# The merged sweep's five picks placed further apart in a chunk, and the comparisons for the next chunk moved into its middle

## The chip, the cores and the metric

The kernel runs on one core of one Trainium2 chip. The metric is the time of one execution on the device in microseconds (us). TensorE (PE in the rows) does matmuls, VectorE (DVE) and ScalarE (ACT) elementwise work, GpSimd (POOL) issues the indirect gathers, SyncE (SP) the plain transfers.

## What is computed

A graph of 6250 nodes and 100000 edges, sorted by their target node, goes through four layers, each followed by a residual sum and a layer norm: a spline network with its convolution, three attention layers, two graph convolutions, and three hops of neighbour means. The change lies in the spline convolution at the end of the first layer. For every edge the edge's place is shifted by the difference of a value of its two nodes and clipped, and the eight corners of the cell that it falls into are weighted:

```python
new_pseudo = jnp.clip(pseudo + t[col] - t[row], 0.0, 1.0)
basis2, idx2 = spline_basis(new_pseudo)
return spline_conv(x, row, col, basis2, idx2, conv_w, conv_b)
...
z = jnp.einsum('ni,kio->nko', x, W).reshape(N * K, Fout)
gathered = z[col[:, None] * K + idx]
msg = jnp.einsum('es,eso->eo', basis, gathered)
out = jax.ops.segment_sum(msg, row, num_segments=N)
```

## The kernel before

Edges lie as 128 partitions times 784 columns. The stage of the change, `stage_conv_sweep`, does two things at a time over chunks of 14 columns (`ch`), two chunks (ring buffers, `b` 0 and 1) a step, 28 steps, so 56 chunks.

**The sweep proper.** GpSimd issues 14 indirect gathers a chunk (line 1885) that fetch each edge's block of the table `z_conv` into `ring[b]`. VectorE multiplies four pairs of corners with their weights (line 2164), adds them up in three steps (2175 and 2176, 2186 and 2187, 2197: the sums), adds the carry of the chunk before (2199) and runs a scan along the columns (2212). ScalarE writes the result out. After the sums VectorE frees the ring (`ring_free`); ScalarE then copies the indices of the chunk two further on (`stage`, 1959), and GpSimd, which waits for them on line 1883, gathers into the ring again.

**The look-up, three steps ahead.** For each edge the value t of one of its nodes is fetched by one-hot products. VectorE makes two one-hot tiles for a chunk (`make`, two comparisons: `hot_lo`, line 2030, and `hot_hi`, 2032). The 14 columns of a chunk are done in five units of three (the last of two). For a unit TensorE counts and turns the one-hots (`turn`, 1910 and 1911), ScalarE copies the turned rows (`take_rows`, 1950), TensorE multiplies them with the table in three parts (`look`, 1920), and VectorE picks the wanted column out of the product (`pick`, 2039, which waits on line 2038). Two result banks alternate, so look u needs pick u-2 to be over (`found_free`). TensorE's order in a chunk is written out: turn 0; then for each row copy that is ready, turn u and look u-1. ScalarE's order in a chunk: the five row copies, the staging of the next indices, the corner weights, then, after the scan (`sums_ready`), the decay factors, the copy out, and the next chunk's row copies.

A third thread, the edge's new place (`place_...`: lines 2046 to 2097), is cut into small steps that stand between the others on VectorE; in even chunks it begins with a long sum (2046).

VectorE's order is written out in `chunk` (2136 on). Ahead of the loop, six chunks of look-ups run alone (`looks_of`), while the first 28 gathers go. The loop has 50 chunks with look-ups; six chunks without follow. Before the change the one-hots are made at the end of a chunk, for the chunk two further on, into the tiles that this chunk's picks have just left.

Of the kernel before, what the change touches and what calls it, by code (L numbers as in the profile page):

```python
# [8 lines left out]
ALU = mybir.AluOpType  # L9
# [5 lines left out]
P = 128  # L15


def gnn_stack_kernel(nc, t, out, stop=None):
# [41 lines left out]
    def sem(name):  # L60
        if name not in sems:
            sems[name] = ctx.enter_context(nc.semaphore(name))
        return sems[name]
# [32 lines left out]
    with ctx:  # L96
# [20 lines left out]
        dve_step, act_step, pe_step, pool_step = (sem(n) for n in ("dve_step", "act_step", "pe_step", "pool_step"))  # L117
# [1704 lines left out]
        def stage_conv_sweep(z, units_, tt, spread, pseudo, key, deg, keep, run, tail):  # L1822
# [10 lines left out]
            with ExitStack() as st, nc.Block() as block:  # L1833
# [71 lines left out]
                def _(pe):  # L1905
# [34 lines left out]
                    pe.wait_ge(sem("hot_made"), 2)  # L1940
                    pe.sem_inc(sem("hot_made"), -2)
# [74 lines left out]
                def _(v):  # L2016
# [12 lines left out]
                    def make(parity, col):  # L2029
                        v.tensor_tensor(hot_lo[parity][:, :, :], short[:, bass.ds(col, ch)].unsqueeze(1).to_broadcast([P, P, ch]),  # L2030
                                        number[:, :, :], ALU.is_equal)
                        v.tensor_tensor(hot_hi[parity][:, :, :], digits[:, bass.ds(col, ch)].unsqueeze(2).to_broadcast([P, ch, NT]),
                                        iota[:, 0:NT].unsqueeze(1).to_broadcast([P, ch, NT]), ALU.is_equal).then_inc(sem("hot_made"), 1)
# [8 lines left out]
                    def pick_on(b, u):  # L2042
                        pick(b, u).then_inc(sem("found_free"), 1)
# [102 lines left out]
                    def chunk(it, b, looks, places):  # L2146
# [15 lines left out]
                        for n in range(4):  # L2162
                            wgt = wgt8[b][:, :, 2 * n:2 * n + 2].unsqueeze(3).to_broadcast([P, ch, 2, fo])
                            last = v.tensor_tensor(acc[n] if n < 2 else pair[n], pair[n], wgt, ALU.mult)
                        last.then_inc(dve_step, 1)
# [5 lines left out]
                        if looks:  # L2171
                            pick_on(b, 0)
                        v.wait_ge(dve_step, 1)
# [8 lines left out]
                        if looks:  # L2182
                            pick_on(b, 1)
# [9 lines left out]
                        if looks:  # L2193
                            pick_on(b, 2)
# [4 lines left out]
                        v.scalar_tensor_tensor(sums[b][:, :, 0], tail[:, :], keep[:, bass.ds(col, 1)], sums[b][:, :, 0], ALU.mult, ALU.add).then_inc(dve_step, 1)  # L2199
                        if places:  # L2200
                            if b == 0:
                                place_cell(1)
                            else:
                                place_index(0, place_col)
                        if looks:
                            pick_on(b, 3)
# [3 lines left out]
                        v.sem_inc(sem("decay_ready"), -1)  # L2210
                        flat = sums[b][:, :, :].rearrange("p f j -> p (f j)")
# [6 lines left out]
                        if looks:  # L2218
                            pick_on(b, 4)
# [3 lines left out]
                        v.tensor_copy(tail[:, :], sums[b][:, :, ch - 1]).then_inc(dve_step, 1)  # L2223
# [5 lines left out]
                        v.wait_ge(dve_step, 1)  # L2229
                        v.sem_inc(dve_step, -1)  # L2230
                        if looks:
                            make(b, look_col + (2 + b) * ch)
                        if places:
                            if b == 0:
                                place_share(1)
                            else:
                                place_end(place_col)

# [5 lines left out]
                    make(1, AHEAD * GR + ch)  # L2244
# [1258 lines left out]
```

## Time and profile before

| | us |
|---|---|
| median of 3 runs | 11738.81 |
| lowest and highest run | 11734.01, 11827.18 |
| profiled execution | 11728.26 |
| its span | 11726.5 |
| VectorE busy in the span | 5526.4 |
| GpSimd busy in the span | 6027.4 |
| TensorE busy in the span | 3555.6 |

The stage of the change takes some 1400 us of the span, from 5107 to 6510; the chain of work through it is what is read below. A row of the order of time gives the start from the beginning of the span and the duration in us, the engine, the line, the operation, output and inputs, and in brackets how long the engine was idle before it and what ended that. "DVEq L2038" is VectorE's own queue at line 2038, which waits there.

### The profile page before, as it was taken

The page shows a single profiled execution, that of the slowest core. Times are in us where ns is not written, and L with a number is a line of the kernel's source. Part 1 is how long each engine was busy: PE and PEld are TensorE (multiplying, and loading weights), DVE is VectorE, ACT ScalarE, POOL GpSimd, SP SyncE. Part 2 cuts the span into 40 slices and gives each one's busy share as a digit, 9 for nine tenths or more (in the row PEclk, how much of TensorE's full clock was granted, in tenths as well). Part 3 has the DMA queues.
Part 4 walks back from the last instruction along what each step waited for, and adds up shares of the span by engine and source line. Part 5 has one row for each costly group of instructions (what it writes and reads, how often), then busy time and mean ns, then how long its engine had stood idle before and what let it go on. Part 6 is the DMA issues. An engine that isn't in the chain of part 4 may idle for free. (4 is left out here: it accounts for less than half of the span.)

```text
span 11726.5 us, 86679 instructions
## 1 busy us (share of the span) xinstructions
PE 3555.6 (30%) x19657; PEld 2292.8 (20%) x19713; DVE 5526.4 (47%) x8114; ACT 2549.8 (22%) x3835; POOL 6027.4 (51%) x6000
## 2 busy tenths in 40 slices
PE   4334310266344443343332100010000200036787
PEld 3222200243111111132222100010000100023554
DVE  5333358444666666557677322222222588871201
ACT  0212125244233333211111011110111244430000
POOL 1555557400565666536656577757776566640000
PEclk8555555588555555555555555555555555558899
DMA  7000012299799999725555111111111132328798
GB/s 297 2 2 2 2 44 103 91 390 391 299 368 357 370 366 369 271 56 143 145 142 151 46 35 32 34 26 36 34 32 33 38 99 99 99 70 310 284 412 356
DMA packets 582791, 1887.74 MB, mean 161 GB/s; under 512 B 253627, under 2 KB 315490, under 8 KB 552065
## 3 DMA queue, kind: packets, MB, share of 16 engines
q0 software_dynamic: 305264, 762.32, 20.7%
q1 hardware_dynamic: 234592, 722.30, 15.9%
q10 hardware_dynamic: 42784, 401.43, 8.2%
q8 instruction: 55, 0.90, 0.0%
q14 instruction: 96, 0.79, 0.0%
HBM read 1170.21 MB, written 715.38 MB: 161 GB/s over the span
## 5 line engine op out<-in xcount | busy, mean ns | idle before, releaser
L2314 POOL DMA_INDIRECT ring<-tab_gat,at x2352 | 2348.5, 999 | 902.3 <-issue 851.9
L735 POOL DMA_INDIRECT ring<-z_stn,at x784 | 761.5, 971 | 1293.3 <-POOLq L742 758.0
L580 POOL DMA_INDIRECT sorted<-rows,at x784 | 799.7, 1020 | 777.1 <-POOLq L578 540.8
L1558 PE MATMUL pair_acc<-pair_x_w,pair_cell 32*112 32x384 f32 (+1 forms) x1120 | 781.0, 879 | 1128.2 <-remote 489.1
L1885 POOL DMA_INDIRECT ring<-z_conv,at x784 | 806.5, 1029 | 599.4 <-POOLq L1883 367.4
L2893 PE MATMUL acc<-spot,ones 128*128 128x128 f32 x6 | 2.3, 487 | 3419.3 <-PEq L2282 2243.7
L1305 PE MATMUL acc<-tile,parts 128*96 128x448 f16 (+1 forms) x3430 | 727.6, 361 | 251.6 <-DVE parts L1229 138.7
L2425 DVE COPY peak<-peak 128x6 f32<-128x6 f32 x112 | 20.0, 179 | 1557.9 <-DMA ring<-tab_gat,at 1341.9
L2893 PEld LDWEIGHTS acc<-spot,ones 128*128 128x128 f32 x6 | 1.5, 310 | 3420.0 <-issue 3420.0
L1558 PEld LDWEIGHTS pair_acc<-pair_x_w,pair_cell 32*112 32x112 f32 x1120 | 317.1, 295 | 1591.1 <-issue 1584.4
L2349 ACT ACTIVATE weights_bank<-arg 128x168 f32<-128x168 f32 (+1 forms) x112 | 31.3, 279 | 2391.3 <-issue 2000.1
L2461 DVE TENSOR_TENSOR_SCAN sums<-decay,sums 128x1176 f32<-128x1176 f32 (+1 forms) x112 | 517.3, 4619 | 29.0 <-issue 15.8
L1305 PEld LDWEIGHTS acc<-tile,parts 128*96 128x96 bf16 (+1 forms) x3430 | 404.3, 125 | 568.9 <-DMA tile<-adj 233.5
L743 POOL DMA_INDIRECT adj<-pair_val,pair_at x392 | 412.0, 1051 | 193.5 <-issue 103.5
L2448 DVE TENSOR_TENSOR sums<-ring,weights_bank 128x1008 f32<-128x1008 f32 (+1 forms) x112 | 430.0, 3839 | 133.7 <-issue 96.7
L1138 POOL DMA_INDIRECT adj<-val_a,at_a x392 | 387.4, 988 | 189.9 <-issue 127.3
L1211 POOL DMA_INDIRECT own<-tab_gcn,ex_src x5 | 5.6, 1120 | 905.5 <-DMA tab_gcn<-hop 599.9
L1676 PE MATMUL planes<-wsb,turned 64*128 64x384 f32 (+1 forms) x1960 | 420.9, 557 | 124.8 <-PEq L1672 116.2
L1693 DVE COPY block<-planes 128x384 f32<-128x384 f32 x588 | 296.0, 552 | 335.1 <-DVEq L1712 335.1
L2364 ACT COPY out_rows<-sums 128x1176 f32<-128x1176 f32 (+1 forms) x112 | 443.0, 3955 | 48.7 <-ACTq L2363 18.6
L1920 PE MATMUL found<-parts,lo_rows 128*128 128x147 bf16 x2352 | 322.0, 313 | 392.9 <-PEq L1917 322.1
L1595 ACT COPY pair_block<-pair_acc 112x384 f32<-112x384 f32 (+1 forms) x896 | 380.0, 501 | 239.9 <-ACTq L1591 107.6
(540 smaller groups left out, 10202.4 us busy)
## 6 DMA issues: line engine op xcount, KB each, us to landing
tile<-adj SPq DMA_DIRECT2D x490, 784.0 KB, 21.4
z_stn<-block ACTq DMA_DIRECT2D x98, 2400.0 KB
z_conv<-pair_block ACTq DMA_DIRECT2D x224, 700.0 KB
run_gat<-out_rows SPq DMA_DIRECT2D x56, 1596.0 KB
adj<-zero SPq DMA_DIRECT2D x49, 1568.0 KB
run_basis<-out_rows SPq DMA_DIRECT2D x28, 1750.0 KB
ring<-tab_gat,at POOLq DMA_INDIRECT x2352
run_gat<-out_rows SPq DMA_DIRECT2D x56, 672.0 KB
```

The source lines that it names most:

```text
L580: g.indirect_dma_start(out=dest, out_offset=bass.IndirectOffsetOnAxis(ap=at[b][:, k:k + 1], axis=0), in_=rows[b][:, k, :], in_offset=None) ...
L735: g.indirect_dma_start(out=view(bufs[b], k), out_offset=None, in_=table, in_offset=bass.IndirectOffsetOnAxis(ap=at[n][b][:, k:k + 1], axis ...
L743: g.indirect_dma_start(out=adj, out_offset=bass.IndirectOffsetOnAxis(ap=pair_at[b][:, k // 2:k // 2 + 1], axis=0), in_=pair_val[b][:, k // ...
L1138: g.indirect_dma_start(out=adj, out_offset=bass.IndirectOffsetOnAxis(ap=at_a[:, k:k + 1], axis=0), in_=val_a[:, k:k + 1], in_offset=None). ...
L1305: ins = pe.matmul(acc[0:3 * w, b, 0:HW_B], parts[:, t_, :, :].rearrange("p k f -> p (k f)"), self.ring[n % RING][:, b * HW_B:(b + 1) * HW_ ...
L1558: last = pe.matmul(self.acc[g][0:self.nodes, n, 0:(hi - lo) * self.fo], self.cell[:, :], cols, start=True, stop=True)
L1676: ins = pe.matmul(self.acc[g][:, n, 0:(hi - lo) * self.fo], self.turned[rows, k, :], cols, start=True, stop=True)
L1885: g.indirect_dma_start(out=ring[b][:, k, :, :, :].rearrange("p u s o -> p (u s o)"), out_offset=None, in_=z, in_offset=bass.IndirectOffset ...
L2314: g.indirect_dma_start(out=ring[b][:, k, :], out_offset=None, in_=tab_gat, in_offset=bass.IndirectOffsetOnAxis(ap=at[b][:, k:k + 1], axis= ...
L2364: a.copy(out_rows[b][:, :, 0:n_sums], sums[b][:, :, :, :].rearrange("p h f j -> p j (h f)"))
L2448: v.tensor_tensor(sums[b][:, :, 1:per_head, :], val_of(ring[b]), ex.unsqueeze(2).to_broadcast([P, NH, width, ch]), ALU.mult)
L2461: v.tensor_tensor_scan(flat, decay[:, :, :, :].rearrange("p h f j -> p (h f j)"), flat, 0.0, ALU.mult, ALU.add).then_inc(dve_step, 1)
```

## The change

VectorE's order in `chunk` is written anew; nothing is computed otherwise, and the four other engines keep their order (TensorE's last wait takes one announcement of one-hots instead of two). The one-hots are made for the next chunk instead of the one after it, in front of the scan instead of at the chunk's end; the pair that stood ahead of the loop for the second chunk goes. The picks move: pick 0 stands after two of the four multiplications, pick 1 after the other two, pick 2 behind the sums, pick 3 behind the one-hots, pick 4 behind the scan's announcement.

```diff
@@ -1937,8 +1937,8 @@
                     with pe.Fori(0, steps):
                         for b in range(2):
                             chunk(b)
-                    pe.wait_ge(sem("hot_made"), 2)
-                    pe.sem_inc(sem("hot_made"), -2)
+                    pe.wait_ge(sem("hot_made"), 1)
+                    pe.sem_inc(sem("hot_made"), -1)
                     pe.matmul(counts_, none[:, :], hot_hi[0][:, 0, :], start=False, stop=True).then_inc(sem("all_counted"), 1)
 
                 @block.scalar
@@ -2159,10 +2159,9 @@
                         acc = [near[:, :, n, :, :] for n in range(2)]
                         if places and b == 0:
                             place_sum()
-                        for n in range(4):
-                            wgt = wgt8[b][:, :, 2 * n:2 * n + 2].unsqueeze(3).to_broadcast([P, ch, 2, fo])
-                            last = v.tensor_tensor(acc[n] if n < 2 else pair[n], pair[n], wgt, ALU.mult)
-                        last.then_inc(dve_step, 1)
+                        wgt = [wgt8[b][:, :, 2 * n:2 * n + 2].unsqueeze(3).to_broadcast([P, ch, 2, fo]) for n in range(4)]
+                        v.tensor_tensor(acc[0], pair[0], wgt[0], ALU.mult)
+                        v.tensor_tensor(acc[1], pair[1], wgt[1], ALU.mult)
                         if places:
                             if b == 0:
                                 place_add(place_col)
@@ -2170,6 +2169,10 @@
                                 place_share(0)
                         if looks:
                             pick_on(b, 0)
+                        v.tensor_tensor(pair[2], pair[2], wgt[2], ALU.mult)
+                        v.tensor_tensor(pair[3], pair[3], wgt[3], ALU.mult).then_inc(dve_step, 1)
+                        if looks:
+                            pick_on(b, 1)
                         v.wait_ge(dve_step, 1)
                         v.sem_inc(dve_step, -1)
                         v.tensor_tensor(acc[0], acc[0], pair[2], ALU.add)
@@ -2179,8 +2182,6 @@
                                 place_sub(place_col)
                             else:
                                 place_two()
-                        if looks:
-                            pick_on(b, 1)
                         v.wait_ge(dve_step, 1)
                         v.sem_inc(dve_step, -1)
                         v.tensor_tensor(acc[0][:, :, 0, :], acc[0][:, :, 0, :], pair[3][:, :, 0, :], ALU.add)
@@ -2190,24 +2191,26 @@
                                 place_clip()
                             else:
                                 place_weights(place_col)
-                        if looks:
-                            pick_on(b, 2)
                         v.wait_ge(dve_step, 1)
                         v.sem_inc(dve_step, -1)
                         step(v.tensor_tensor(sums[b][:, :, :].rearrange("p f j -> p j f"), acc[0][:, :, 0, :], pair[3][:, :, 1, :], ALU.add))
                         v.sem_inc(sem(f"ring_free{b}"), 1)
                         v.scalar_tensor_tensor(sums[b][:, :, 0], tail[:, :], keep[:, bass.ds(col, 1)], sums[b][:, :, 0], ALU.mult, ALU.add).then_inc(dve_step, 1)
+                        if looks:
+                            pick_on(b, 2)
                         if places:
                             if b == 0:
                                 place_cell(1)
                             else:
                                 place_index(0, place_col)
                         if looks:
-                            pick_on(b, 3)
+                            make(1 - b, look_col + (1 + b) * ch)
                         v.wait_ge(dve_step, 1)
                         v.sem_inc(dve_step, -1)
                         v.wait_ge(sem("decay_ready"), 1)
                         v.sem_inc(sem("decay_ready"), -1)
+                        if looks:
+                            pick_on(b, 3)
                         flat = sums[b][:, :, :].rearrange("p f j -> p (f j)")
                         v.tensor_tensor_scan(flat, decay[:, :, :].rearrange("p f j -> p (f j)"), flat, 0.0, ALU.mult, ALU.add).then_inc(dve_step, 1)
                         if places:
@@ -2215,33 +2218,30 @@
                                 place_cell(2)
                             else:
                                 place_index(1, place_col)
-                        if looks:
-                            pick_on(b, 4)
                         v.wait_ge(dve_step, 1)
                         v.sem_inc(dve_step, -1)
                         v.sem_inc(sem("sums_ready"), 1)
-                        v.tensor_copy(tail[:, :], sums[b][:, :, ch - 1]).then_inc(dve_step, 1)
                         if places:
                             if b == 0:
                                 place_cell(3)
                             else:
                                 place_index(2, place_col)
-                        v.wait_ge(dve_step, 1)
-                        v.sem_inc(dve_step, -1)
                         if looks:
-                            make(b, look_col + (2 + b) * ch)
+                            pick_on(b, 4)
+                        v.tensor_copy(tail[:, :], sums[b][:, :, ch - 1]).then_inc(dve_step, 1)
                         if places:
                             if b == 0:
                                 place_share(1)
                             else:
                                 place_end(place_col)
+                        v.wait_ge(dve_step, 1)
+                        v.sem_inc(dve_step, -1)
 
                     make(0, 0)
                     for n in range(AHEAD):
                         looks_of(n)
                         if n + 1 < AHEAD:
                             places_of(n)
-                    make(1, AHEAD * GR + ch)
                     with v.Fori(0, steps - AHEAD) as it:
                         for b in range(2):
                             chunk(it, b, True, True)
```

The row numbers of lines differ by one or a few in the changed kernel; the names are the same (`found_245` and `found_246` are the two result banks, `hot_hi_222` and `hot_hi_223` the one-hots of even and odd chunks, `ring_236` and `sums_238` belong to the odd chunk). VectorE's first half of an odd chunk in the loop, from the multiplications to the additions of pairs, before:

```order
L2164 TENSOR_TENSOR corner_banks<-ring_236,corner_banks 128x14x64 x2
L2164 TENSOR_TENSOR ring_236<-ring_236,corner_banks 128x14x64 x2
L2072 TENSOR_SCALAR share<-share 128x84
L2039 TENSOR_TENSOR prod<-found_246,hot_hi_223 128x441
L2175 TENSOR_TENSOR corner_banks<-corner_banks,ring_236 128x14x64
L2176 TENSOR_TENSOR ring_236<-corner_banks,ring_236 128x14x64
L2076 TENSOR_TENSOR two<-share 128x112
L2039 TENSOR_TENSOR prod<-found_245,hot_hi_223 128x441
```

The same place in the changed kernel:

```order
L2163 TENSOR_TENSOR corner_banks<-ring_236,corner_banks 128x14x64
L2164 TENSOR_TENSOR corner_banks<-ring_236,corner_banks 128x14x64
L2072 TENSOR_SCALAR share<-share 128x84
L2039 TENSOR_TENSOR prod<-found_246,hot_hi_223 128x441
L2172 TENSOR_TENSOR ring_236<-ring_236,corner_banks 128x14x64
L2173 TENSOR_TENSOR ring_236<-ring_236,corner_banks 128x14x64
L2039 TENSOR_TENSOR prod<-found_245,hot_hi_223 128x441
L2178 TENSOR_TENSOR corner_banks<-corner_banks,ring_236 128x14x64
L2179 TENSOR_TENSOR ring_236<-corner_banks,ring_236 128x14x64
```

Picks 0 and 1 (line 2039) each moved up past two large operations. VectorE's second half of an odd chunk, from the weights of the third thread to the chunk's last row copies, before:

```order
L2091 TENSOR_TENSOR w_231<-two,share 128x224
L2039 TENSOR_TENSOR prod<-found_246,hot_hi_223 128x441
L2197 TENSOR_TENSOR sums_238<-corner_banks,ring_236 128x14x32
L2199 ISA
L2199 SCALAR_TENSOR_TENSOR sums_238<-conv_tail,keep_s,sums_238 128x32
L2081 ISA
L2081 SCALAR_TENSOR_TENSOR spot<-cell,base 128x28
L2039 TENSOR_TENSOR prod<-found_245,hot_hi_223 128x441
L2212 SCALAR_TENSOR_TENSOR sums_238<-decay,sums_238 128x448
L2084 SCALAR_TENSOR_TENSOR spot<-cell,spot 128x28
L2039 TENSOR_TENSOR prod<-found_246,hot_hi_223 128x294
```

After these stand the carry's copy (2223) and the two comparisons, there for `hot_lo_221` and `hot_hi_223`, the odd chunk's own tiles. The same place in the changed kernel:

```order
L2196 TENSOR_TENSOR sums_238<-corner_banks,ring_236 128x14x32
L2198 ISA
L2198 SCALAR_TENSOR_TENSOR sums_238<-conv_tail,keep_s,sums_238 128x32
L2039 TENSOR_TENSOR prod<-found_246,hot_hi_223 128x441
L2081 ISA
L2081 SCALAR_TENSOR_TENSOR spot<-cell,base 128x28
L2030 ISA
L2030 TENSOR_TENSOR hot_lo_220<-short_b,number_b 128x1792
L2032 ISA
L2032 TENSOR_TENSOR hot_hi_222<-digits,iota 128x686
L2039 TENSOR_TENSOR prod<-found_245,hot_hi_223 128x441
L2215 SCALAR_TENSOR_TENSOR sums_238<-decay,sums_238 128x448
```

Pick 2 moved from ahead of the sums to behind them, and the comparisons, now for the next (even) chunk's tiles, stand between pick 2 and pick 3, ahead of the scan (line 2215).

## Rows read from the trace of the kernel before

**Rows 1.** Windows: length; PE, PEld, DVE, ACT, POOL busy; clock, DMA; then L2030 alone.

```profile
5223.00:6396.00 1173.00, 387.99 (x3424) 337.55 (x3424) 827.51 (x1301) 208.22 (x441) 709.93 (x687) 0.54 0.51 144
6396.00:6505.00 109.00, 0.20 (x1) 0.10 (x1) 67.61 (x92) 11.07 (x21) 69.17 (x70) 0.50 0.56 160
...
5223.00:6396.00 1173.00, 53.52 (x49) 0.54 0.51 144
```

**Rows 2.** Waits, 5223 to 6396: who for whom; us in total, times, longest.

```profile
POOL ring L1885 <- POOLq L1883: 314.4, 50, 54.2
...
DVE prod L2039 <- DVEq L2038: 287.4, 57, 9.6
```

**Rows 3.** Order of time, VectorE, an even chunk, its successor's beginning and pick 2.

```profile
5543.70 2.08 DVE L2164 TENSOR_TENSOR ring<-ring,corner_banks 128x896 f32<-128x896 f32 x2
...
5545.85 0.61 DVE L2039 TENSOR_TENSOR prod<-found,hot_hi 128x441 f32<-128x441 f32 x1
...
5548.52 0.62 DVE L2039 TENSOR_TENSOR prod<-found,hot_hi 128x441 f32<-128x441 f32 x1
...
5550.11 0.20 DVE L2058 TENSOR_SCALAR moved<-moved 128x84 f32<-128x84 f32 x1
5554.91 0.62 DVE L2039 TENSOR_TENSOR prod<-found,hot_hi 128x441 f32<-128x441 f32 x1 [4.60 <-DVEq L2038]
5555.45 0.91 DVE L2197 TENSOR_TENSOR sums<-corner_banks,ring 128x448 f32<-128x448 f32 x1
...
5557.00 0.61 DVE L2039 TENSOR_TENSOR prod<-found,hot_hi 128x441 f32<-128x441 f32 x1
5557.53 1.08 DVE L2212 TENSOR_TENSOR_SCAN sums<-decay,sums 128x448 f32<-128x448 f32 x1
...
5559.61 1.09 DVE L2030 TENSOR_TENSOR hot_lo<-short_b,number_b 128x1792 bf16<-128x1792 bf16 x1 [0.24 <-DVEq L2230]
...
5561.41 0.24 DVE L2070 SCALAR_TENSOR_TENSOR share<-moved,cell 128x84 f32<-128x84 f32 x1
...
5579.18 0.62 DVE L2039 TENSOR_TENSOR prod<-found,hot_hi 128x441 f32<-128x441 f32 x1 [8.84 <-DVEq L2038]
```

**Rows 4.** Order of time, TensorE, looks 0 to 2 of the odd chunk.

```profile
5562.28 1.32 PE L1920 MATMUL found<-parts,lo_rows 128*128 128x147 bf16 x9
...
5563.84 1.22 PE L1920 MATMUL found<-parts,lo_rows 128*128 128x147 bf16 x9
...
5566.42 0.75 PE L1920 MATMUL found<-parts,lo_rows 128*128 128x147 bf16 x9 [0.95 <-DVE prod L2039]
```

**Rows 5.** Order of time, GpSimd, first, second and last gather, next first.

```profile
5533.73 1.51 POOL L1885 DMA_INDIRECT ring<-z_conv,at  x1 [5.39 <-POOLq L1883]
5535.54 1.85 POOL L1885 DMA_INDIRECT ring<-z_conv,at  x1 [0.30 <-issue]
...
5551.45 0.94 POOL L1885 DMA_INDIRECT ring<-z_conv,at  x1 [0.30 <-issue]
5557.95 1.42 POOL L1885 DMA_INDIRECT ring<-z_conv,at  x1 [5.56 <-POOLq L1883]
```

**Rows 6.** The gathers' line, 5133 to 5170: ns min/median/max, first and last start.

```profile
L1885 POOL DMA_INDIRECT ring<-z_conv,at x28: 942/946/1325, 5133.2 to 5167.3; - x28
```

**Rows 7.** Order of time, VectorE, the four picks that follow, ahead of the loop.

```profile
5137.74 0.62 DVE L2039 TENSOR_TENSOR prod<-found,hot_hi 128x441 f32<-128x441 f32 x1 [1.10 <-DVEq L2038]
5143.51 0.62 DVE L2039 TENSOR_TENSOR prod<-found,hot_hi 128x441 f32<-128x441 f32 x1 [5.15 <-DVEq L2038]
5156.23 0.62 DVE L2039 TENSOR_TENSOR prod<-found,hot_hi 128x441 f32<-128x441 f32 x1 [12.10 <-DVEq L2038]
5169.52 0.47 DVE L2039 TENSOR_TENSOR prod<-found,hot_hi 128x294 f32<-128x294 f32 x1 [12.67 <-remote]
```

**Rows 8.** Order of time, ScalarE, row copies 0 and 4 of the odd chunk.

```profile
5561.10 0.48 ACT L1950 CAST lo_rows<-turned 128x384 bf16<-128x384 f32 x1 [0.35 <-ACTq L1949]
...
5579.92 0.37 ACT L1950 CAST lo_rows<-turned 128x256 bf16<-128x256 f32 x1 [8.08 <-ACTq L1949]
```

## The prediction

> **What bounds the kernel now.** The change touches one stage, the merged sweep of the first graph layer, so I read that stage alone: first busy times by stretch, then the waits inside it, then single chunks in order of time. The loop that the change rewrites takes 1173 us for 49 chunks [rows 1], 23.94 us each, and VectorE is busy for 827.51 us of it, 16.9 us a chunk. In the list of waits VectorE's largest is the pick, 287.4 us in 57 waits that line 2038 ends, where it waits for a look (the product on TensorE) to be announced; GpSimd waits 314.4 us for its indices, 54.2 of them before the loop's first chain of gathers [rows 2], so 5.3 us a chunk. Neither engine is full, and each chunk loses some 6 us of VectorE in front of a pick.
>
> The order of time tells which pick, and why. In the chunk at 5543 picks 0 and 1 come without a wait (5545.85 and 5548.52), and pick 2 starts after 4.60 us of idleness, at 5554.91; in the next chunk pick 2 waits 8.84 us, to 5579.18 [rows 3]. Yet TensorE's row of look 2 in that chunk ends at 5566.42 + 0.75 = 5567.17 [rows 4]: it is announced 12 us after its row. What ends the wait is seen on GpSimd: the first gathers of the two chains start at 5533.73 and 5557.95, and the two late picks start 21.18 and 21.23 us after them, 2.5 us after the last of the 14 gathers (5551.45 + 0.94 = 5552.39) [rows 3, 5]. The stretch before the loop shows the same beside an idle VectorE: 28 gathers run from 5133.2 to past 5167.3 [rows 6], 1.26 us apart, and picks that only follow one another come at 5137.74, 5143.51, 5156.23 and 5169.52 [rows 7], that is 4.5, 10.3, 23.0 and 36.3 us after the first gather, with up to 12.67 us of waiting, where the rows of two looks in a row are 1.56 us apart (5562.28, 5563.84) [rows 4]. I read from this: **TensorE's announcements pass at once in the first 6 us or so after a chain of gathers has begun, are held afterwards with one let through now and then, and all pass about 21.2 us after its first gather.** That is the bound of a chunk: gathers, release, what is left on VectorE, the next gathers.
>
> That row and announcement differ is nothing odd in itself. The Trainium skill, "Perfetto Trace Analysis", section "Per-instruction lifecycle: what the profiler-reported window actually captures", says that a matmul's end in a profile is an estimate, while its semaphore follows PSUM's acknowledgement; the 12 us agree with the order, but no page read gives a reason for the size.
>
> **The change, part by part.**
>
> *Work.* The loop issues the same instructions a chunk. One pair of comparisons less runs ahead of the loop, 1.80 us (5559.61 to 5561.41) [rows 3]: -2 us.
>
> *Picks.* Now picks 0, 1 and 2 stand before the sums (line 2197) that free the ring and so let ScalarE stage the next indices; after, only picks 0 and 1 do. If looks came at the same times as now, the wait of pick 2 would no longer hold the ring.
>
> *The comparisons, from behind the scan to before it.* They and pick 2 will stand between the freeing of the ring and the scan. Now it is 1.55 us from the start of the sums to pick 3 (5555.45 to 5557.00), 0.91 of them the sums, then pick 3 0.53 and the scan 1.08 [rows 3]. After: 0.64 + pick 2 0.53 + a gap of 0.24 + comparisons 1.80 + pick 3 0.53 + scan 1.08 = 4.82 us from the end of the sums to the end of the scan. The next first gather comes 1.59 us after the sums (5556.36 to 5557.95) [rows 3, 5]. So the scan will end 3.2 us after the first gather; now it is 5558.61 - 5557.95 = 0.66 us. **This step decides.** ScalarE waits for the scan, copies the chunk out, and only then turns to the next chunk's row copies: copy 0 starts 2.49 us after the scan (5558.61 to 5561.10) [rows 3, 8], and every look of the next chunk stands behind it.
>
> *Where the looks fall then.* Now copy 0 is 3.15 us after the first gather, look 0's row ends 2.5 us after the copy's start (5562.28 + 1.32 = 5563.60), and look 1's 1.5 us later [rows 4]: 5.6 and 7.1 us after the first gather, in time for VectorE; look 2 ends 9.2 us after it and is held to 21.2. After the change copy 0 comes at 3.2 + 2.49 = 5.7, look 0 at 8.2 and look 1 at 9.7 or later: both in the held stretch. Bounds: let through in the middle, as what released the pick at 10.3 [rows 7], or held to 21.2, as look 2 now. Turn 1 and look 0 are issued before turn 2 and look 1, and in rows 7 the next one to pass after 10.3 passed at 23.0. So I take look 0 in the middle and look 1 held.
>
> *A chunk then.* Pick 1 at 21.2; the pick, two additions and a placing step as from pick 0 to pick 1 now, 2.67 us (5545.85 to 5548.52); the two half additions, 1.59 - 0.53 = 1.06 (5548.52 to 5550.11, less a pick); a placing step 0.20 and the sums 0.91 [rows 3]: 4.84. Then 1.59 to the next first gather. 21.2 + 4.84 + 1.59 = 27.6 us; and since the ring sets the gathers again, the next scan ends 3.2 us after them too, so the state keeps itself up. Against 23.94 that is +3.66, times 49 = **+179 us**.
>
> *The comparisons beside the gathers.* Now the gather that meets them takes 1.85 us where others take 0.95 [rows 5]. After, they start about 1.4 us after the sums and still run into the first two gathers, so these 0.9 us stay; were they to fall away, it would be 49 x 0.9 = 44 us less. The Trainium skill, "SBUF — State Buffer", section "Who interferes with whom", infers that a two-input VectorE operation leaves descriptor generation alone; the 1.85 us beside one speak against it. By the rule the 44 us could not be in the sum at all, and moving the comparisons would be free.
>
> *Sum.* Span 11726.5 + 179 - 2 = 11903.5; 1.8 us lie around the span (11728.26). The median of the runs is 10.6 above the profiled one, so **11915 us**, +1.5%.
>
> **The rivals.**
>
> 1. *Look 0 is held to the end too* (the 23.0 in rows 7 speaks for it, the 10.3 against). Pick 0 at 21.2 and 0.53, two multiplications 2.08 [rows 3], pick 1 at 23.8: a chunk of 30.2, +6.3 x 49 = +307: 12040 us.
>
> 2. *Look 1 is let through in mid-chunk.* Then the ring is free early and the row copies set the pace: copy 4 comes with the release (0.7 us after the pick in its chunk, 5579.92 to 5579.18 [rows 3, 8], or with it), its 0.37 and 1.59 us of staging follow: 23.2 to 23.9 a chunk, 0 to 0.7 less than now: 11700 to 11740, or up to 11810 where look 1 passes only at 19 us (19 + 4.84 + 1.59 = 25.4 a chunk). For it: something passes in mid-chunk now as well, or copy 4 would come later than the release; against it: look 1 is the fourth thing issued, not the second.
>
> 3. *Faster:* the hold hangs on how TensorE and VectorE alternate, not on the gathers, and spreading the picks dissolves it. Then gathers set the chunk: in the last six chunks, which have no looks, 109 us or 18.2 each [rows 1], or 14 x 1.26 + 2 = 19.6. (23.94 - 19.6) x 49 = -213: 11525 us. Against it stand rows 7, where VectorE does nothing and the hold is there. It is decided by look 2: out by 14 us after the first gather, or not. The same section of the Trainium skill says that TensorE and ScalarE never wait on anyone, which would be this case; the held picks show that the announcements do wait, if not at SBUF's ports.
>
> **How the numbers follow.** Look 1 held: 0.50. Rival 1: 0.12. Rival 2: 0.29. Rival 3: 0.09. About 1% (117 us, 2.4 us a chunk) is what a measurement of this kernel can tell from no change: the first two cases lie beyond it (0.62), rival 2 within. The range from 11700 to 12040 leaves out rival 3 and what exceeds rival 1. The likeliest case alone has 11855 to 11980 (look 1 out at 20 to 22.5 us).
>
> **What would show it.** In the trace after: VectorE's wait moves from pick 2 to pick 1 (the pick behind line 2173), about 10 us long, ending 21 us after the first gather; the scan ends some 3 us after the first gather; GpSimd's wait for indices grows from 5.3 to some 9 us a chunk; picks 2 to 4 have no wait. I am wrong if the scan ends less than 2 us after the first gather, or if looks whose rows end 8 to 10 us after the first gather are announced at once.

## The result, and the profile after

The changed kernel takes 11897.42 us (median of 3 runs, 11892.09 to 11920.31) against 11738.81: 158.6 us more. The ratio over the runs is 1.0102, 95% interval 1.0057 to 1.0147, so it is slower, by less than 2%; it lies below that of the medians (1.0135) because the three runs of before spread over 93 us. Timed a second time, beside the experiments, it was 1.0155 (1.0118 to 1.0191).

The profiled execution of after is the longest of its three (11920.31 us, span 11918.5). Its span is 192.0 longer than that of before: 158.7 of it between the first and the last gather of the merged sweep (1511.7 us, before 1353.0), 7.8 ahead of it, 25.5 behind it, where the two programs are the same. The sweep's share comes out at the difference of the medians; that it does so to a tenth of a us is chance, since these are single executions. In the second pair of traces the sweep is 145.3 us longer (1477.8 and 1332.5).

The loop of after, by windows (columns as in [rows 1]), and the waits inside it:

```profile
5230.00:6561.00 1331.00, 397.95 (x3424) 341.21 (x3424) 836.77 (x1298) 207.86 (x441) 675.75 (x686) 0.53 0.46 127
```

```profile
POOL ring L1885 <- POOLq L1883: 496.6, 49, 52.8
DVE prod L2039 <- DVEq L2038: 388.5, 80, 9.4
```

1331 us in place of 1173 [rows 1] for 49 chunks: 27.2 us each, while VectorE's work hardly grew (836.77 against 827.51). GpSimd's waits for indices went from 5.3 to 9.2 us a chunk ((496.6 - 52.8) / 48), VectorE's waits for a look from 287.4 [rows 2] to 388.5 us.

One odd chunk in order of time, VectorE (start, length, line, out<-in, idle before and what ended it):

```profile
5552.28 0.92 DVE L2196 TENSOR_TENSOR sums<-corner_banks,ring 128x448 f32<-128x448 f32 x1
...
5553.73 0.61 DVE L2039 TENSOR_TENSOR prod<-found,hot_hi 128x441 f32<-128x441 f32 x1
...
5554.36 1.08 DVE L2030 TENSOR_TENSOR hot_lo<-short_b,number_b 128x1792 bf16<-128x1792 bf16 x1
5555.36 0.87 DVE L2032 TENSOR_TENSOR hot_hi<-digits,iota 128x686 bf16<-128x686 f32 x1
5556.15 0.61 DVE L2039 TENSOR_TENSOR prod<-found,hot_hi 128x441 f32<-128x441 f32 x1
5556.67 1.08 DVE L2215 TENSOR_TENSOR_SCAN sums<-decay,sums 128x448 f32<-128x448 f32 x1
...
5566.66 0.62 DVE L2039 TENSOR_TENSOR prod<-found,hot_hi 128x441 f32<-128x441 f32 x1 [5.05 <-DVEq L2038]
...
5575.28 0.62 DVE L2039 TENSOR_TENSOR prod<-found,hot_hi 128x441 f32<-128x441 f32 x1 [6.01 <-DVEq L2038]
...
5579.41 0.92 DVE L2196 TENSOR_TENSOR sums<-corner_banks,ring 128x448 f32<-128x448 f32 x1
```

The same chunk on GpSimd (first, second and last gather, next first), ScalarE (row copies 0 to 3) and TensorE (looks 0 and 1):

```profile
5554.79 1.48 POOL L1885 DMA_INDIRECT ring<-z_conv,at  x1 [9.21 <-POOLq L1883]
5556.57 0.95 POOL L1885 DMA_INDIRECT ring<-z_conv,at  x1 [0.30 <-issue]
...
5571.55 0.94 POOL L1885 DMA_INDIRECT ring<-z_conv,at  x1 [0.30 <-issue]
5581.80 1.58 POOL L1885 DMA_INDIRECT ring<-z_conv,at  x1 [9.31 <-POOLq L1883]
```

```profile
5560.23 0.48 ACT L1950 CAST lo_rows<-turned 128x384 bf16<-128x384 f32 x1 [0.35 <-ACTq L1949]
5561.75 0.48 ACT L1950 CAST lo_rows<-turned 128x384 bf16<-128x384 f32 x1 [1.04 <-ACTq L1952]
5573.07 0.48 ACT L1950 CAST lo_rows<-turned 128x384 bf16<-128x384 f32 x1 [10.84 <-ACTq L1949]
5575.33 0.48 ACT L1950 CAST lo_rows<-turned 128x384 bf16<-128x384 f32 x1 [1.78 <-ACTq L1949]
```

```profile
5561.42 1.32 PE L1920 MATMUL found<-parts,lo_rows 128*128 128x147 bf16 x9
...
5562.98 1.12 PE L1920 MATMUL found<-parts,lo_rows 128*128 128x147 bf16 x9
```

What to see: the scan ends at 5557.75, 2.96 us after the first gather (before 0.66); copy 0 starts at 5.4. Looks 0 and 1 end at 5562.74 and 5564.10 by their rows, 7.95 and 9.3 us after the first gather. Pick 0 gets its look at 11.9 and pick 1 at 20.5 us, 11 us after look 1's row and 2.8 us after the last gather's end (5572.49). (In the even chunks pick 0 waits less: a median 1.6 us, against 3.6 in the odd.) Behind pick 1 come the sums, and 1.5 us behind these the next gathers: 27.0 us. Picks 2 to 4 wait for nothing, here and in every other chunk of the loop.

### The profile page after: what moved, and what is told of

The parts are those of the page before. It is cut to its first block and busy times, and to the rows that moved or that the text cites. A ratio compares the mean times of both kernels' runs of the same rounds, so it can differ in the third digit from the quotient of the medians.

```text
span 11918.5 us, 86677 instructions
## 1 busy us (share of the span) xinstructions
PE 3576.1 (30%) x19657; PEld 2303.2 (19%) x19713; DVE 5535.9 (46%) x8112; ACT 2549.3 (21%) x3835; POOL 6000.1 (50%) x6000
## 3 DMA queue, kind: packets, MB, share of 16 engines
q0 software_dynamic: 305264, 762.32, 21.2%
q1 hardware_dynamic: 234592, 722.30, 15.6%
## 5 line engine op out<-in xcount | busy, mean ns | idle before, releaser
L1885 POOL DMA_INDIRECT ring<-z_conv,at x784 | 772.7, 986 | 792.1 <-POOLq L1883 558.9
L2364 ACT COPY out_rows<-sums 128x1176 f32<-128x1176 f32 (+1 forms) x112 | 443.1, 3956 | 48.7 <-ACTq L2363 15.6
## 6 DMA issues: line engine op xcount, KB each, us to landing
tile<-adj SPq DMA_DIRECT2D x490, 784.0 KB, 21.4
```

Source lines behind the costliest of these rows:

```text
L1885: g.indirect_dma_start(out=ring[b][:, k, :, :, :].rearrange("p u s o -> p (u s o)"), out_offset=None, in_=z, in_offset=bass.IndirectOffset ...
L2364: a.copy(out_rows[b][:, :, 0:n_sums], sums[b][:, :, :, :].rearrange("p h f j -> p j (h f)"))
```

## The experiments

**My theory:** GpSimd's chain of gathers holds TensorE's announcements; the change makes the looks late against the chain, because the scan ends later. **Rivals:** the picks' new places cost it by themselves; the hold comes from the bytes moved, or from how TensorE and VectorE alternate. The experiments ran on several chips (the kernel before took 11640 to 11769 us there), so ratios are against the kernel before timed beside each; they all differ from 1 by some 2% or less, and what counts is whether the interval leaves out 1. Chunk means are of the profiled execution, from the sums of one chunk on VectorE to the sums of the next.

### Is it the gathers? Seven of them, and none (e5, e6)

```
e5:  for k in range(7): g.indirect_dma_start(...)          # was range(ch), 14
   + g.dma_start(ring[b][:, 7:ch], z[0:P*7*(KD+2), :] in pieces of one gathered row)
e6:  no indirect gather; one g.dma_start for all 14
```

> The changed kernel with seven indirect gathers a chunk in place of 14; the other seven rows of a chunk come by one plain transfer of the same size and the same pieces from fixed rows, issued by GpSimd behind them (their indices are left out of the computation). My theory: the hold goes with GpSimd's chain of gathers, so it ends some 2.8 us after the seventh: 7 x 1.25 + 0.5 + 2.8 = 12 us after the first gather in place of 20.5, and a chunk is 12 + 4.84 + 1.59 = 18.4 us or what VectorE's 17.6 us of work and short waits make it, up to 20; about 11430 to 11520 us with the last six chunks shorter too. The rivals: the hold goes with the bytes moved or with how TensorE and VectorE alternate: pick 1 stays some 20 us after the first gather, 27 us a chunk, 11850 or more.

> The changed kernel with all 14 gathers of a chunk replaced by one plain transfer of the same bytes in the same pieces from fixed rows (the indices are left out of the computation). My theory: without indirect gathers no announcement is held; every look is out within 0.5 us of its row's end, no pick waits over 3 us, and VectorE's work sets the chunk, 17.6 to 20 us: 11400 to 11520 us. If it is the bytes that hold TensorE, picks still wait 5 us or more while the transfer runs. If TensorE's rows are simply shown too early and the looks take that long by themselves, the picks wait as in the changed kernel, 27 us a chunk.

Measured: 11527.6 and 11433.07 us, one run each, beside one of 11769.23 for the kernel before. A chunk is 20.1 and 18.9 us; e5 lies just above what was expected of it (11520 us, 20 us a chunk), e6 within. VectorE's waits for looks in the loop (who for whom, us, times, longest), first e5, then e6, and the window of e6:

```profile
DVE prod L2041 <- DVEq L2040: 87.1, 24, 3.7
```

```profile
DVE prod L2038 <- DVEq L2037: 30.7, 24, 1.3
```

```profile
5195.00:6105.00 910.00, 364.14 (x3360) 317.95 (x3360) 816.54 (x1272) 203.58 (x432) 51.99 (x48) 0.58 0.51 181
```

388.5 us of waiting became 87.1 and 30.7, and VectorE is busy 816.54 of 910 us in e6: it now sets the chunk. The bytes do not hold TensorE: e6 moves 181 GB/s where the changed kernel moves 127. Nor do TensorE and VectorE by themselves: their work and order are unchanged. For every turn and look of the loop I took the time from the end of its row to the change of its semaphore in the trace, grouped by when the row ended, in us after the chain's first gather (in e6 after the transfer's issue); count: median/longest:

```
       0 to 4         6 to 8         8 to 10           10 to 14        14 to 20       20 to 24
after  96: 0.01/0.02  72: 0.04/3.80  120: 10.08/12.31  1: 8.43/8.43    51: 3.95/7.42  131: 0.01/0.47
e5     96: 0.01/0.02  72: 0.03/2.41  120:  1.68/2.08   129: 0.01/0.02  63: 0.01/0.02  -
e6     96: 0.01/0.02  48: 0.01/0.02  128:  0.01/0.26   175: 0.01/0.26  33: 0.01/0.02  -
```

The same instructions at the same distance are late by 10.08, 1.68 and 0.01 us with 14, 7 and 0 gathers. (Nine rows of after end later than 24 us; they are late by 0.02 at most.) A chunk of e5, GpSimd's seventh gather and VectorE's picks 0 and 1 (first gather at 5523.11):

```profile
5531.16 0.95 POOL L1885 DMA_INDIRECT ring<-z_conv,at  x1 [0.30 <-issue]
```

```profile
5533.53 0.62 DVE L2041 TENSOR_TENSOR prod<-found,hot_hi 128x441 f32<-128x441 f32 x1 [3.62 <-DVEq L2040]
5536.06 0.61 DVE L2041 TENSOR_TENSOR prod<-found,hot_hi 128x441 f32<-128x441 f32 x1
```

Pick 0 comes 1.4 us after the seventh gather's end, pick 1 without a wait. The theory stands for what holds. What in the gathers does it, no run shows: GpSimd's work of issuing them, their packets (in the trace of after the last of a chain ends a median 0.4 us before look 1 is announced), or their completions, one for each gather where the plain transfer has one for all. Nor does a run show whether the product itself or only its announcement is late: a row's end is modelled, and TensorE goes on with its next rows meanwhile (turn 2 starts at 5562.53 in the chunk shown above, with look 0 not announced before 5566.5).

### Which part of the change costs? (e1, e2, e3)

```
e1 (after):   make(1-b) taken from ahead of the scan; make(b), two chunks ahead, at the end
e2 (before):  make(b) taken from the end; make(1-b), one chunk ahead, ahead of the scan
e3 (after):   pick 2, make, pick 3 moved from ahead of the scan to behind it
```

> The changed kernel, but with the comparisons back at the chunk's end, two chunks ahead; the picks stay where the change puts them. My theory: what costs is that the scan ends 3 us after the first gather. Here 1.8 us of comparisons leave the stretch between the sums and the scan, so the scan ends 1.2 to 1.4 us after the first gather, copy 0 comes at 3.7 to 3.9, look 0's row ends at 6.3 and look 1's at 7.8. Look 0 still passes at once, look 1 is the first or the second announcement that is held: out at 11.7 or 18.2 us after the first gather (as looks 0 and turn 2 in the changed kernel), so the ring is free early or at 23.0; a chunk of 23.3 to 24.6 us, 11710 to 11790 us. The rival, that the places of the picks cost it and not the comparisons: a chunk stays at 27.0 us and the time at 11900.

> The kernel before with its picks, but the comparisons between the sums and the scan, one chunk ahead. My theory: the scan ends 2.5 to 3 us after the first gather, all looks come as late as in the changed kernel, look 1 is announced at 20.5 us and look 2 only 1 to 1.5 us behind it; pick 2 stands before the sums, so a chunk is 21.5 to 22 + 0.5 + 0.9 + 1.6 = 24.5 to 25.0 us, up to 27 where pick 1 at 20.5 has the two half additions behind it too; 11770 to 11890 us, slower than before in any case. The rival, that the places of the picks alone cost it: 23.9 us a chunk, 11740.

> The changed kernel with its two picks ahead of the sums and one-ahead comparisons, but the scan straight behind the sums and picks 2 to 4 and the comparisons behind the scan. My theory: the scan ends 0 to 0.5 us after the first gather or before it, copy 0 comes at 3 us or earlier, looks 0 and 1 pass at once as in the kernel before, nothing held stands in front of the sums; the ring is free at about 15 us, and the next indices wait only for ScalarE's row copy 4 (turn 4, at about 21): first gather at 23.2 to 23.9, 11700 to 11740 us, no slower than before and 160 to 200 us faster than the changed kernel. The rival, that two picks ahead of the sums cost it wherever the scan is: 27 us a chunk, 11900.

| run | ratio to before (95%) | chunk (sums to sums): mean, shortest to longest | scan's end after the first gather, median |
|---|---|---|---|
| before, two traces | 1 | 23.94, 21.3 to 25.1; 23.55, 17.8 to 36.2 | 0.66; 0.66 |
| after, again | 1.0155 (1.0118 to 1.0191) | 26.5, 24.1 to 27.0 | 2.97 |
| e1 | 1.0035 (1.0022 to 1.0048) | 24.0, 15.7 to 44.8 | 0.89 |
| e2 | 1.0092 (1.0064 to 1.0121) | 25.2, 24.6 to 25.6 | 2.45 |
| e3 | 1.0000 (0.9978 to 1.0021) | 23.15, 18.0 to 36.2 | -3.7 |

A chunk of e3 in a steady stretch, its first gather, scan and the next first gather (the scan ends at 5640.81, 3.45 us ahead of that gather):

```profile
5622.25 1.13 POOL L1885 DMA_INDIRECT ring<-z_conv,at  x1 [4.65 <-POOLq L1883]
5639.72 1.09 DVE L2209 TENSOR_TENSOR_SCAN sums<-decay,sums 128x448 f32<-128x448 f32 x1 [0.16 <-issue]
5644.26 1.33 POOL L1885 DMA_INDIRECT ring<-z_conv,at  x1 [4.58 <-POOLq L1883]
```

The comparisons ahead of the scan cost 0.9% by themselves, the picks' places 0.35%. With both but the scan moved forward (e3) nothing is lost: the rival on the picks' places is wrong for the most part, and what costs is the late scan. By their means all three came out as expected (e2 0.2 us above the 24.5 to 25.0 given first, e3 just below 23.2), but not in their course. From sums to sums, chunks of 24 us did not stay 24:

```
after   27.0 27.0 27.1 27.0 27.1 27.1 28.6 27.0 27.0 27.0 27.0 26.9 27.1 27.0 28.5
e1      18.3 27.8 18.9 28.5 18.9 29.2 15.7 26.6 27.7 22.3 21.6 27.7 18.2 30.4 15.7
e3      18.7 29.4 18.7 22.1 20.8 23.5 18.3 27.6 19.4 24.9 20.8 23.5 20.8 23.5 18.0
before  19.8 26.2 21.1 24.8 22.6 24.0 22.0 24.8 23.3 24.0 24.0 24.0 24.0 24.0 19.9
```

(the last line is the second trace of before). Most of this is not the clock of the loop: the sums move inside a chain, according to which look is held, while ScalarE stages the next indices only behind row copy 4, whose turn mostly comes with the release. In the first six chunks of e1 above, the sums start some 16 and some 21 us after the first gather by turns, but the first gathers lie 22.6 to 24.2 us apart. From first gather to first gather the loop of the second trace of before has 22.8 to 24.1 us in all but four of its 49 chunks, and e3 21.9 to 26.6. A chunk grows much longer where a chain follows the one ahead almost at once: three chains in these traces (two in the second of before, one in e1) begin 0.3 to 2.1 us after the last gather, in place of some 5. Row copy 0 then comes 6.8, 20.8 and 21.7 us after the first gather, in place of some 3, and these chunks take 27.7, 35.3 and 39.9 us.

e3 has steady stretches of 22.0 to 22.4 and chunks of up to 26.6, and its mean is 0.4 to 0.8 below before's two traces, 20 to 39 us, of which the times show nothing. For the second trace of before I expected

> The kernel before, unchanged, for a second trace of it beside the others of this call. My theory: the same chunk as in the first trace, 23.9 us; if a chunk here is 23.0 to 23.3, single executions of the kernel before differ by as much as the scan-first kernel gains.

(11695.04 us, 23.55 us a chunk: single executions of before differ by half of what e3 has on the first), and for that of after

> The changed kernel, unchanged, timed beside the others. 27.0 us a chunk again, and 1.010 to 1.016 times the kernel before.

(26.5 us a chunk where 27.0 was expected, and a ratio of 1.0155.)

### Trying to keep the gain (e4, e7 to e10)

e3's steady 22.1 us a chunk invite edits that start the next gathers right with the release, or bring copy 0 sooner.

```
e4 (e3):   ScalarE: wait turned(4); [ring_free; stage]; copy 4            # stage was behind copy 4
e7 (e3):   ScalarE: copy 3; [ring_free; weights; decay; copy-out]; wait turned(4); copy 4; stage
e8 (e7):   stage ahead of copy 4, as in e4
e9 (e3):   GpSimd: ahead of gather 7 of 14 wait for ScalarE's row copy 1;  e10: for row copy 3
```

> The kernel of e3 with one edit on ScalarE: the next indices are staged when turn 4 is announced, ahead of row copy 4, not behind it. My theory: the release of turn 4 at 20.5 to 21.2 us after the first gather then sets the next gathers 1.2 us later: a chunk of 21.7 to 22.4 us, 75 to 110 us less than the kernel before: 11630 to 11665 us. If instead the announcements are held longer when the gathers follow one another more closely (as ahead of the loop, one in 12.7 us), turn 4 comes later and the chunk is 24 us or more: 11740 or above.

> The kernel of e3 with ScalarE's weights, decay, copy-out ahead of the wait for turn 4, where ScalarE stands idle, and the next indices behind row copy 4 as in e3. In e3's trace a chunk alternates: 22.1 us where looks 0 and 1 come early, and 27 to 36 where copy 0 came late and they were held. Here copy 0 of the next chunk has only row copy 4 and the staging ahead of it on ScalarE, and turn 0: 1.0 to 1.5 us after the first gather in place of 2.1 in e3. My theory (announcements pass in the first 6 us): looks 0 and 1 pass in nearly every chunk, chunks of 22.0 to 22.5 with every eighth 1.4 us longer, mean 22.3 to 23.0: 0.992 to 0.998 times the kernel before. If the hold does not go by the time since the first gather, the long chunks stay: mean 23.1 and no less than e3's time.

> The kernel of e7 with the next indices staged when turn 4 is announced, ahead of row copy 4, as in e4. The first gather then comes 0.5 to 0.7 us sooner after the release, and copy 0 1.6 to 2.1 us after it. My theory: chunks of 21.5 to 22.0 where looks 0 and 1 still pass, mean 21.7 to 22.8, 0.990 to 0.997 times the kernel before; if that 0.6 us already makes them late, as e4 against e3, long chunks of 29 to 32 come back and the mean is 24: 1.00 or above.

> The kernel of e3 with one edit: after the seventh gather of a chain GpSimd waits until ScalarE has made row copy 1 of the running chunk. My theory (the hold ends 2.6 us after a chain's last gather, and only then): where copy 1 has passed early nothing changes; where it is held, seven gathers end at 8.8 us, turn 1 is announced at 11.4, the second seven run from 11.9 to 20.7, and the looks pass in the 6 us from 11.4 on; the ring is free at about 20 and the next chain begins at 21.3 to 22: mean chunk 21.3 to 22.8, 0.983 to 0.996 times the kernel before. If a pause inside the chain ends no hold, each chunk is some 3 us longer: 24 to 27 us, 1.00 to 1.02 times.

> The kernel of e9 with the pause in the middle of a chain tied to row copy 3, which the traces show held, not to copy 1, which mostly passes early. My theory (a hold ends some 2.6 us after GpSimd's last gather, also of half a chain): seven gathers end 9 us after the first, turn 3 is announced at 11 to 12 us, the second seven run until 20.7 to 21.5, turn 4 and the looks pass in the 6 us from 11.4 on, the ring is free at about 16 to 20 and the next chain follows at once: mean chunk 21 to 22.5 us, 0.983 to 0.996 times the kernel before. If a pause inside the chain ends no hold, GpSimd stands until one announcement is let through in mid-chain: 24 to 29 us a chunk, 1.00 to 1.03.

Measured, ratio to before and mean chunk: e4 1.0043 (1.0025 to 1.0062), 24.2; e7 1.0098 (1.0062 to 1.0135), 24.7; e8 1.022 (1.0181 to 1.0259), 27.8; e9 1.0031 (1.0013 to 1.0049), 23.9; e10 1.0004 (0.9991 to 1.0017), 23.5. None beats the kernel before, and e4, e7, e8 and e10 miss the gain that was expected of them.

e4, first gathers of three chains, and ScalarE's copies 0 to 3 of the chunk between the last two with the stage behind them:

```profile
5404.66 1.58 POOL L1885 DMA_INDIRECT ring<-z_conv,at  x1 [5.27 <-POOLq L1883]
5426.47 1.11 POOL L1885 DMA_INDIRECT ring<-z_conv,at  x1 [3.93 <-POOLq L1883]
5453.09 1.13 POOL L1885 DMA_INDIRECT ring<-z_conv,at  x1 [9.26 <-POOLq L1883]
```

```profile
5429.48 0.48 ACT L1952 CAST lo_rows<-turned 128x384 bf16<-128x384 f32 x1 [0.71 <-ACTq L1949]
5430.99 0.48 ACT L1952 CAST lo_rows<-turned 128x384 bf16<-128x384 f32 x1 [1.04 <-ACTq L1954]
5437.32 0.48 ACT L1952 CAST lo_rows<-turned 128x384 bf16<-128x384 f32 x1 [5.85 <-ACTq L1949]
5446.57 0.48 ACT L1952 CAST lo_rows<-turned 128x384 bf16<-128x384 f32 x1 [8.77 <-ACTq L1949]
5451.95 0.20 ACT L1961 COPY at<-cells 128x14 int32 x1 [4.90 <-ACTq L1960]
```

The first chunk is 21.8 us, as expected. The gathers then stand 0.7 us nearer to the last release than in e3, copy 0 is 3.0 us behind the first of them (2.1 there), turn 2 is held, pick 1 comes with the release at 20.05 us, and the stage comes 0.4 us behind the sums (they end at 5451.51), as in the changed kernel: 26.6 us. The gain of one chunk is the loss of the next.

e7 failed in part by my own placing. ScalarE's row copies 3 and 4 and the stage:

```profile
5403.14 0.48 ACT L1952 CAST lo_rows<-turned 128x384 bf16<-128x384 f32 x1 [12.92 <-ACTq L1951]
...
5405.39 0.96 ACT L1993 COPY out_rows<-sums 128x448 f32<-128x448 f32 x1 [0.28 <-ACTq L1992]
5406.70 0.37 ACT L1952 CAST lo_rows<-turned 128x256 bf16<-128x256 f32 x1 [0.35 <-ACTq L1951]
5407.34 0.20 ACT L1961 COPY at<-cells 128x14 int32 x1 [0.27 <-ACTq L1954]
```

Turn 3 is often held as well, and then copy 3 comes with the release; the 3 us of work that I had put between copies 3 and 4 for an idle stretch start only then, and the next chain begins 6.7 us after the last gather (4.6 in e3's steady stretch). The larger part lies elsewhere. In each of the six eighth chunks (see the last section) row copy 4 comes at 15.2 to 15.6 us and the next chain begins 0.3 us after the last gather. There is no pause between the two; row copy 2 of the chunk that this chain opens comes only at 20.8 to 24.5 us (at 5 to 7 in most), and the chunk takes 34.6 to 42.5 us from first gather to first gather. These six pairs of chunks hold 58 of the 73 us by which e7's loop is longer than e3's. In e8's chunks of 30.6 us, pick 1 is held to 20.0 us, the sums end at 24.9, and the stage comes 4.6 us behind them, since weights, decay and copy-out now stand ahead of it; in e4 it comes 0.4 us behind them.

In e9 the pause never came about inside the loop: copy 1 had always been made by the seventh gather, so it tells nothing of the theory. In e10 it did. GpSimd's seventh and eighth gather, and ScalarE's copies 2 and 3:

```profile
5422.95 0.95 POOL L1888 DMA_INDIRECT ring<-z_conv,at  x1 [0.30 <-issue]
5429.12 0.94 POOL L1888 DMA_INDIRECT ring<-z_conv,at  x1 [5.23 <-POOLq L1887]
```

```profile
5426.04 0.48 ACT L1953 CAST lo_rows<-turned 128x384 bf16<-128x384 f32 x1 [9.46 <-ACTq L1952]
5427.56 0.48 ACT L1953 CAST lo_rows<-turned 128x384 bf16<-128x384 f32 x1 [1.04 <-ACTq L1952]
```

Copy 2, held for 9.46 us, goes 2.1 us after the seventh gather's end (5423.90), with seven more to come: a pause of GpSimd ends the hold, with the same gathers and the same bytes still to do. The time is no better, because the pause (5.2 us here) is paid in nearly every chunk: it only moves from between two chains (a median 5.4 us in before, 0.3 in e10) into the middle of one.

## Why the prediction was right

11915 us was forecast, +1.5%, with 11700 to 12040; 11897.42 came.

- *The step that decides held.* Scan 3.2 us after the first gather: 2.96. Copy 0 at 5.7: 5.4. Look 0's row at 8.2: 7.95; look 1's at 9.7 or later: 9.3. e1 to e3 show that it is this step: undoing it takes most or all of the loss away.
- *Look 0 in the middle, look 1 held to the end* (the 0.50 case): 11.9 and 20.5 us. Rival 1 (look 0 held too) and rival 2 (look 1 in mid-chunk) did not come up in the trace; in the second trace of after pick 1 came before the release, at 17.5 to 19.5 us, in the eighth chunks and most of those behind them. Rival 3, the faster one, is refuted by e5 and e6.
- *Behind pick 1*: 4.84 us to the end of the sums and 1.59 to the next gather forecast; 5.05 and 1.47 in the chunk shown.
- *One term was mis-sized: the comparisons beside the gathers.* The 0.9 us were to stay. In the chunk shown the second gather takes 0.95 in place of 1.85 [rows 5], since the comparisons now meet the first gather of the chain, and they end before the second begins. The prediction's own terms said so: comparisons from 1.4 to 3.2 us after the sums, a first gather from 1.6 to 3.0, the second at 3.3. The first gather takes 1.47 to 1.58 beside them; in before it took a median 1.42 beside the scan and a pick, so little is added there (in e8, with neither, it takes 0.94). A chain is 17.8 us long where it was 18.65 (medians), and the release comes at 20.5, not 21.2. That is the 0.6 us between 27.6 and 27.0. Over 49 chunks it makes 29 us less (the text gave 44 for a full 0.9 us each), and the six eighth chunks (below; five of about 28.5 us, one of 27.7) make 8 more: the loop grew by 159.6 us (1172.8 to 1332.5) where 179 were forecast.
- *Waits:* VectorE's on pick 1 was put at about 10 us; it is 6.0 in the chunk shown (medians 7.4 in odd chunks, 4.6 in even), since pick 0 waits ahead of it (3.6 and 1.6); GpSimd's was put at some 9 us a chunk and is 9.2.
- *What is luck:* that the forecast lies within 18 us. Three executions of after spread over 28 us and three of before over 93, and in the second pair of traces the loop grew by only 145.8 us (1153.9 to 1299.7), with 26.5 us a chunk.
- *What the prediction had not seen:* it took a chunk of before for a steady 23.94 us. By first gathers that holds for its trace (22.9 to 24.9), but the second trace has one chunk of 27.7 and one of 35.3, where two chains came close. The changed kernel has none of these, because there the ring, and with it the next chain, always waits for the release.

## What to carry to other kernels

Where a busy engine's waits end long after the row of the work waited for, measure everything from what the other queues started last: here the first gather of a chain, not the chunk, was the clock. Moving work into a gap is free only if nothing behind it is on the way to the next producer; the 1.8 us of comparisons sat ahead of a scan that ScalarE, and through it TensorE, waited for. And a loop whose buffers couple one turn to the next has to be judged by the mean of many turns: a turn made 2 us shorter may only make the next one 12 us longer (20.8 and 35.3 us in the second trace of before, where most have about 23).

## What the hardware showed unexpectedly

- TensorE's announcements are late by up to 12 us while GpSimd issues indirect gathers, by 0.26 at most while a plain transfer moves the same bytes; a pause of GpSimd ends it 1.4 to 2.8 us after its last gather (2.8 in the chunk shown of after, 2.1 in e10, 1.4 in e5).
- Every eighth chain of 14 gathers has 1.72 us between its first and second gather in place of 0.30 (1.78 in before, 1.6 to 2.3 in e1 to e4 and e7 to e9, 3.3 to 3.5 in e10); none of e5's chains of seven has such a gap. In the trace of after that chunk mostly takes 28.5 us in place of 27.0:

```profile
5391.26 1.48 POOL L1885 DMA_INDIRECT ring<-z_conv,at  x1 [9.39 <-POOLq L1883]
5394.45 0.94 POOL L1885 DMA_INDIRECT ring<-z_conv,at  x1 [1.72 <-issue]
```

No run shows why, nor is the gap the whole of it: in the second trace of after it is there too (1.71), and the eighth chunks take 24.1 to 25.5 us there. In e10, from sums to sums, the eighth chunks are among the shortest, 17.7 us, and those behind them the longest, up to 36.6; from first gather to first gather they are 21.4 to 23.4 and up to 29.3.
